# A graph layer on one core: the target list is loaded ahead of a row tile, its search is split in two sums, and the end of the last feature tile is dealt out anew

## The reference

```
h   = relu(layernorm(x))                      # x is (1250, 512)
xn  = batchnorm(h, g1, b1)
agg = segment_sum(xn[src], dst) / max(deg, 1)
conv = relu(agg @ W_conv + b_conv)
attn = (phi(q) @ (phi(k).T @ v)) / (phi(q) @ sum(phi(k))) @ Wo     # 8 heads, 256 features, the first 256 nodes
out = x + batchnorm(conv + attn + h, g2, b2)
```

## Time and the profile before

| | us |
|---|---|
| median of 3 runs | 176.44 (176.09 to 176.51) |
| the profiled execution | 176.07 |
| its span in the trace | 174.2 |
| TensorE busy | 165.6 (95%) |
| VectorE busy | 137.9 (79%) |
| ScalarE busy | 89.9 (52%) |

### The profile page before, as it was taken

The page is one execution under the profiler, slowest core; times in us unless marked ns, Lnnn a source line. Parts: engine busy times, 40 slices in busy tenths (PEclk is TensorE's granted clock), DMA queues, the critical chain, the costliest instruction groups (busy, mean ns, idle before and its releaser), DMA issues.

```text
span 174.2 us, 3024 instructions
## 1 busy us (share of the span) xinstructions
PE 165.6 (95%) x1131; PEld 108.9 (63%) x1132; DVE 137.9 (79%) x315; ACT 89.9 (52%) x163; POOL 7.6 (4%) x22
## 2 busy tenths in 40 slices
PE   7899999999999999999999999999999999999960
PEld 2388877545545546557777798684464574767940
DVE  2868889989947786999656785975999998597981
ACT  3426999839694779979416164217600505004050
POOL 5037000000000000000000000000000000000000
PEclk9999999999999999999999999999999999999998
DMA  5997970000610000000000000000294014050046
GB/s 186 362 328 185 346 261 0 0 4 0 218 43 0 4 0 0 0 4 2 0 4 0 0 4 0 0 4 4 70 336 186 0 28 119 6 147 0 4 124 172
DMA packets 11884, 13.71 MB, mean 79 GB/s; under 512 B 1458, under 2 KB 6748, under 8 KB 11868
## 3 DMA queue, kind: packets, MB, share of 16 engines
q1 hardware_dynamic: 10476, 12.13, 21.3%
q10 hardware_dynamic: 1072, 1.10, 1.8%
q0 software_dynamic: 320, 0.26, 0.7%
HBM read 10.92 MB, written 2.56 MB: 77 GB/s over the span
## 4 chain that ended last, share of the span: by engine, by line
PE 88%; DVE 3%; ACT 3%; DMA 2%; issue 1%; DVEq 0%; ACTq 0%
PE bank L978 24%; PE bank L708 20%; PE bank L638 8%; PE bank L659 4%; PE bank L732 4%; PE bank L722 4%; PE bank L751 4%; PE bank L685 4%; PE bank L650 3%; PE bank L630 3%; PE bank L1005 2%; PE bank L696 2%; DMA xs<-in_x 2%; DVE gl L1222 1%; DVE st L1054 1%
## 5 line engine op out<-in xcount | busy, mean ns | idle before, releaser
L978 PE MATMUL bank<-r,gh 128*128 128x512 f16 (+8 forms) x140 | 39.3, 314 | 0.0
L978 PE MATMUL bank<-r,gl 128*128 128x512 f16 (+8 forms) x140 | 39.3, 313 | 0.0
L708 PE MATMUL bank<-wc,xs 128*128 128x512 f32 (+1 forms) x80 | 38.5, 608 | 0.2 <-DVE gl L1222 0.2
L1085 DVE TENSOR_TENSOR ohb<-iota,bcol 128x1280 f16<-128x1280 f16 x25 | 20.5, 818 | 3.7 <-PE bank L650 3.7
L708 PEld LDWEIGHTS bank<-wc,xs 128*128 128x128 f32 (+1 forms) x80 | 13.6, 187 | 11.6 <-issue 11.6
L392 ACT ACTIVATE r<-bank 128x500 f16<-128x500 f32 x25 | 18.3, 764 | 3.4 <-PE bank L650 3.4
L978 PEld LDWEIGHTS bank<-r,gh 128*128 128x128 f16 (+1 forms) x140 | 13.5, 97 | 8.5 <-issue 0.3
L978 PEld LDWEIGHTS bank<-r,gl 128*128 128x128 f16 (+1 forms) x140 | 13.6, 97 | 8.2
L608 ACT ACTIVATE bw<-mv,epst 128x1 f32<-128x1 f32 x4 | 1.2, 295 | 31.0 <-DVE mv L1385 31.0
L638 PE MATMUL bank<-hT,r 128*128 128x256 f32 x64 | 14.5, 381 | 0.0
L650 PEld LDWEIGHTS bank<-ohv,ohb 128*128 128x128 f16 x250 | 9.7, 98 | 6.7 <-issue 5.3
(11 more groups left out here) (177 smaller groups left out, 267.1 us busy)
## 6 DMA issues: line engine op xcount, KB each, us to landing
xs<-in_x SPq DMA_DIRECT2D x15, 256.0 KB, 4.6
out<-xs SPq DMA_DIRECT2D x7, 256.0 KB
r<-in_L_gnn_Wq SPq DMA_DIRECT2D x1, 1024.0 KB, 7.5
r<-in_L_gnn_Wk SPq DMA_DIRECT2D x1, 1024.0 KB, 5.7
wc<-in_L_gnn_W_conv SPq DMA_DIRECT2D x1, 1024.0 KB, 9.1
wvo<-in_L_gnn_Wv SPq DMA_DIRECT2D x1, 1024.0 KB, 11.2
wvo<-in_L_gnn_Wo SPq DMA_DIRECT2D x1, 1024.0 KB, 5.3
xs<-in_x ACTq DMA_DIRECT2D x3, 256.0 KB, 4.2
```

The costliest lines, as they stand in the source:

```text
L708: last = nc.tensor.matmul(acc[0:n, :], xnT[:, f, i * P:i * P + n], wc[:, f, :], start=(f == 0), stop=(f == FT - 1))
L978: last = nc.tensor.matmul(acc[:, 0:cn], gg[0:n, s, f * P:(f + 1) * P], A16[0:n, s, c0:c0 + cn], start=(s == 0 and gg is gh), stop=(s == NT ...
L1085: last = V.tensor_tensor(oh[:, s0:s0 + n, :].rearrange("p s (m t) -> p s m t", t=2), iota16[:, 0:size].rearrange("p (m t) -> p m t", t=2). ...
```

## The change

Five edits at the start, and one at the end:

- ScalarE's queue issues the target list first and then tiles 3 and 5; SP issues tile 1 second, where the target list was. SP waits for tile 7, not 9, before `wk`.
- The thresholds are compared in three pieces: columns 0 to 3 ahead of `ln_stats(0)`, 3 to 5 between `ln_stats(0)` and `ln_scale(0)`, 5 to 10 after tile 1 is normalised. The wait for the target list thus stands ahead of the statistics of tiles 0 and 1.
- TensorE sums columns 0 to 5 between its first constant matmuls (now 15) and one more, and columns 5 to 10 after the turns of tiles 0 and 1; the three constant matmuls ahead of q are gone. VectorE adds the two sums (`first_rows` has three instructions instead of two).
- VectorE scales tile 1 (`normal_second`) without rectifying, and rectifies it as it copies the turned tile out of PSUM (`store_second`). ScalarE does neither for tile 1 any more.
- The last feature tile: VectorE scales columns 0 to 512, ScalarE 512 to 768, 768 to 1024 and 1024 to 1250; the parts of the third tile are turned in the order 2, 0, 1 instead of 1, 2, 0.

```diff
-ROUSE, ROUSE_MORE = 18, 3
+SEARCHED = 5
+ROUSE, ROUSE_LATE = 15, 1
...
-        order = [("hT", 0), ("hT", 1), ("first",), ("q", 0), ...
+        order = [("first",), ("hT", 0), ("hT", 1), ("q", 0), ...
...
-        order_end += [("agg", FT - 1, c) ...] + [("zT", FT - 2, j) for j in (1, 2, 0)]
+        order_end += [("agg", FT - 1, c) ...] + [("zT", FT - 2, j) for j in (2, 0, 1)]
...  SP
             load_x(0)
-            sp.dma_start(edst[:, :], dst...).then_inc(dst_in, 16)
+            load_x(1)
             sp.dma_start(wq, ...)
...
-            sp.wait_ge(x_in[NT - 1], 16)
+            sp.wait_ge(x_in[7], 16)
             sp.dma_start(wk, ...)
...  ScalarE
-            for i in (1, 3, 5):
+            act.dma_start(edst[:, :], dst...).then_inc(dst_in, 16)
+            for i in (3, 5):
                 act.dma_start(xs[:, i, :], x[i * P:(i + 1) * P, :]).then_inc(x_in[i], 16)
...
             ln_tile(0)
-            ln_tile(1)
             store_hT(0)
-            store_hT(1)
...
-                for a, b in (...) if f < FT - 1 else ((0, 256), (256, 512), (1024, N)):
+                for a, b in (...) if f < FT - 1 else ((512, 768), (768, 1024), (1024, N)):
...  TensorE
             rouse(ROUSE)
+            edge_search(0)
+            rouse(ROUSE_LATE)
             pe.wait_ge(id_set, 1)
             transpose_h(0)
             transpose_h(1)
-            edge_search()
-            rouse(ROUSE_MORE)
+            edge_search(1)
...
-            transpose_z(FT - 2, (1, 2))
+            transpose_z(FT - 2, (2,))
             turn_with_residual(FT - 2, 0)
+            transpose_z(FT - 2, (1,))
...  VectorE
+            def normal_second():
+                dve.wait_ge(ln_ready, 1)
+                V.tensor_scalar(xs[:, 1, :], xs[:, 1, :], lnw[:, 2, 1:2], lnw[:, 3, 1:2], ALU.mult, ALU.add).then_inc(n1_ready, 1)
+
+            def store_second():
+                acc = landed(dve, "hT", 1)
+                V.tensor_scalar(hT[:, :, P:2 * P], acc[:, :].rearrange("p (t n) -> p t n", t=FT), 0.0, None, ALU.max
+                                ).then_inc(read("hT", 1), 1)
...
+            dve.wait_ge(dst_in, 16)
+            link(V.tensor_copy(edst2[:, :, :], ...))
+            edge_thresholds(0, 3)
             ln_stats(0)
+            edge_thresholds(3, SEARCHED)
             ln_scale(0)
-            edge_thresholds()
+            normal_second()
+            edge_thresholds(SEARCHED, EJ // GR)
+            store_second()
             first_rows()
...
-                V.tensor_scalar(yT[:, f, 512:1024], yT[:, f, 512:1024], ...
+                V.tensor_scalar(yT[:, f, 0:512], yT[:, f, 0:512], ...
```

More of the change, by code:

```diff
@@ L118, in gnn_kernel @@
         edst2 = r2[0:EP, 1280:1280 + EJ // GR].bitcast(F16).rearrange("p (j t) -> p j t", t=2)
-        first = sb("first", [P, 2], F32)
+        first = sb("first", [P, 4], F32)
         rows = sb("rows", [P, 2], I32)
@@ L188, in gnn_kernel @@
         V_G1, V_B1, V_G2, V_B2, V_BC = range(5)
-        order = [("hT", 0), ("hT", 1), ("first",), ("q", 0), ("q", 1), ("hT", 2), ("hT", 3), ("hT", 4), ("hT", 5),
+        order = [("first",), ("hT", 0), ("hT", 1), ("q", 0), ("q", 1), ("hT", 2), ("hT", 3), ("hT", 4), ("hT", 5),
                  ("consts",), ("k", 0), ("hT", 6), ("hT", 7), ("hT", 8), ("hT", 9), ("dq",), ("k", 1), ("uk", 0), ("uk", 1),
@@ L201, in gnn_kernel @@
             order_end += [("agg", f, 0), ("agg", f, 1)] + [("zT", f - 1, j) for j in range(3)] + [("agg", f, 2)]
-        order_end += [("agg", FT - 1, c) for c in range(len(LAST_CHUNKS))] + [("zT", FT - 2, j) for j in (1, 2, 0)]
+        order_end += [("agg", FT - 1, c) for c in range(len(LAST_CHUNKS))] + [("zT", FT - 2, j) for j in (2, 0, 1)]
         order_end += [("zT", FT - 1, j) for j in range(3)]
@@ L261, in gnn_kernel @@
         h_ready = sem("h_ready")
+        n1_ready = sem("n1_ready")
         rows_ready = sem("rows_ready")
@@ L611, in _ @@
                 act.wait_ge(st2_ready, f + 1)
-                for a, b in ((0, 512), (512, 1024), (1024, N)) if f < FT - 1 else ((0, 256), (256, 512), (1024, N)):
+                for a, b in ((0, 512), (512, 1024), (1024, N)) if f < FT - 1 else ((512, 768), (768, 1024), (1024, N)):
                     act.activation(yT[:, f, a:b], yT[:, f, a:b], ACT.Identity,
@@ L626, in transpose_h @@
             def transpose_h(i):
-                pe.wait_ge(h_ready, i + 1)
+                if i == 1:
+                    pe.wait_ge(n1_ready, 1)
+                else:
+                    pe.wait_ge(h_ready, max(i, 1))
                 acc = pe_open(pe, "hT", i)
@@ L790, in rouse, with edge_search @@
                     nc.tensor.matmul(bank[0][:, :], cone[:, :], cone[:, 0:1].to_broadcast([P, 512]), start=True, stop=True)
-            def edge_search():
-                pe.wait_ge(nb_ready, 1)
-                acc = pe_open(pe, "first")
-                for hf in range(2):
[L796 to L799, removed]
+            def edge_search(half):
+                pe.wait_ge(nb_ready, half + 2)
+                if half == 0:
+                    pe_open(pe, "first")
+                acc = bank[uses[("first",)][0]]
+                a, b = ((0, SEARCHED), (SEARCHED, EJ // GR))[half]
+                for hf in range(2):
+                    for j in range(a, b):
+                        last = nc.tensor.matmul(acc[0:GROWS, 2 * half + hf:2 * half + hf + 1],
+                                                below[:, j, hf * GROWS:(hf + 1) * GROWS], cone[0:EP, 0:1],
+                                                start=(j == a), stop=(j == b - 1))
+                if half:
+                    last.then_inc(full("first"), 1)
             def project_consts():
@@ L1001, in transpose_z @@
                     for i in range(4 * j, min(4 * j + 4, NT)):
-                        if f == FT - 1 and i in (0, 2):
-                            pe.wait_ge(z_act, 3 * f + i // 2 + 1)
+                        if f == FT - 1 and i in (4, 6):
+                            pe.wait_ge(z_act, 3 * f + i // 2 - 1)
                         o = (i - 4 * j) * P
@@ L1088, in one_hots @@
                 last.then_inc(oh_ready, 1)
+            def normal_second():
[5 more added lines that the diff above has]
+                                ).then_inc(read("hT", 1), 1)
             def first_rows():
                 acc = landed(dve, "first")
-                V.tensor_scalar(first[0:GROWS, :], acc[0:GROWS, 0:2], -1.0, 0.0, ALU.add, ALU.max).then_inc(read("first"), 1)
+                V.tensor_copy(first[0:GROWS, :], acc[0:GROWS, 0:4]).then_inc(read("first"), 1)
                 stored(dve, "first")
-                V.tensor_scalar(rows[0:GROWS, :], first[0:GROWS, :], float(ROW_MAX), None, ALU.min).then_inc(rows_ready, 1)
+                link(V.scalar_tensor_tensor(out=first[0:GROWS, 0:2], in0=first[0:GROWS, 0:2], scalar=-1.0, in1=first[0:GROWS, 2:4],
+                                            op0=ALU.add, op1=ALU.add))
+                V.tensor_scalar(rows[0:GROWS, :], first[0:GROWS, 0:2], 0.0, float(ROW_MAX), ALU.max, ALU.min).then_inc(rows_ready, 1)
             def edge_values():
@@ L1242, in attn_norm, with edge_thresholds @@
                                 zr[:, i, :].unsqueeze(2).to_broadcast([P, 4, DH]), ALU.mult).then_inc(read("attn", i), 1)
[L1244 to L1249, removed]
+            def edge_thresholds(a, b):
+                shape = [EP, b - a, NW // 2, 2]
+                V.tensor_tensor(below[:, a:b, :].rearrange("p j (w t) -> p j w t", t=2),
+                                edst2[:, a:b, :].unsqueeze(2).to_broadcast(shape),
                                 thr16[0:EP, :].rearrange("p (w t) -> p w t", t=2).unsqueeze(1).to_broadcast(shape),
@@ L1256, in _ @@
             V.tensor_copy(win0[:, :], wbase_i[:, :])
+            dve.wait_ge(dst_in, 16)
+            link(V.tensor_copy(edst2[:, :, :], edst[:, ::GR].unsqueeze(2).to_broadcast([EP, EJ // GR, 2])))
+            edge_thresholds(0, 3)
             ln_stats(0)
+            edge_thresholds(3, SEARCHED)
             ln_scale(0)
-            edge_thresholds()
+            normal_second()
+            edge_thresholds(SEARCHED, EJ // GR)
+            store_second()
             first_rows()
```

6 lines of the change are left out of this document (3 added, 3 removed).

## The result

| | before | after |
|---|---|---|
| median | 176.16 (20 runs, 175.76 to 177.24) | 176.63 (20 runs, 176.11 to 179.27) |
| the profiled execution, span | 176.07, 174.2 | 178.52, 176.2 |
| mean granted clock of that execution | 0.996 | 0.987 |

A forecast was written before the change was run, and what follows sets the result against it. From the first matmul of q TensorE was taken as the bound, with VectorE's copy gating k. Start -0.88, list wait +1.23 and end -0.33 summed to +0.02, on a median of 176.44: 176.5, range 175.5 to 177.3.

The forecast's parts named there:

- The sum: Whole kernel: the three terms, -0.88 + 1.23 - 0.33, add up to +0.02 us, forecasting a median of 176.5.
- rule of t: Start: with the target list there at t, the first statistics and what follows shift by t - 3.37 us.
- Term 2: Start: waiting for the target list, there at t = 4.6, costs +1.23 us, from +0.1 to +2.1.
- rule of a tenth for a tenth: Start: every tenth of a microsecond by which the target list is late costs a tenth.
- case of the list crowded out: Start: tile 1 and `wq` pass beside the list, t 5.1 to 5.6, about 177.2; 0.30 with clock and lost gain.
- upper case of the prediction: Start: if DMA engines alternate between queues by single pieces, the list is there only at t = 5.5.
- Term 1: Start: were the list free, q could begin 1.19 us earlier and k, gated by VectorE, 0.88 earlier: -0.88.
- Term 3: End: the last residuals and the stores behind them come 0.33 us sooner: -0.33, between -0.1 and -0.45.
- rival of the clock: Start: TensorE's clock falls after some 2.5 us of pauses, lengthening q: +2, about 178.5; 5 in 100.
- `wk` at nothing: Start: `wk`, issued once tile 7 is there, lands sooner than before and stays hidden, costing nothing.

The follow-up runs named there:

- second execution: The changed kernel run once more, unchanged, on the chip of the next experiments: 176.30 (12 runs), ratio 1.0007 to the kernel before; this is its trace.
- filled kernel: Changed kernel with 20 instead of 15 constant matmuls at the start, 6 instead of 1 after the first half search, 1 more before q: 177.16, ratio 1.0064.
- copy moved alone: Kernel before with only VectorE's `query_copy(1)` moved ahead of the scale of tiles 6 to 9: 176.41 against 176.06, ratio 1.000.
- copy ahead with the old end: Changed kernel, old load order, list asked for later, `query_copy(1)` ahead of `ln_scale(2)`, without the edits of the end: 175.51, ratio 0.9949 to the kernel before.
- kernel with the copy ahead: Changed kernel with old load order, list waited for after tile 1's scaling, `query_copy(1)` ahead of `ln_scale(2)`: 175.24 against 176.16, ratio 0.9939.
- list later, new loads: Changed kernel with the list's wait behind `ln_scale(0)` and `normal_second`, both search halves behind the turns: 176.73, ratio 1.0037 to the kernel before.
- list second: Changed kernel with the old load order (list second on SP's queue), its wait still ahead of the first statistics: 179.39, ratio 1.0127 to the kernel before.
- list later, old loads: Changed kernel with the old load order, the list's wait after tile 1's scaling, both search halves behind the turns: 176.03, ratio 1.000 to the kernel before.

## Why the prediction was right, and which of its steps were off

The median of 176.63 stands beside a forecast of 176.5, but its composition is another. Executions whose clock held give 176.41 and 176.23, that is +0.25 and +0.07; the clock's fall adds 1.9 and 1.6 to about one execution in four, and 0.22 to the median of the first 20.

That the number came so near is in good part luck. The sum said +0.02, and +0.47 came. The 176.5 was counted from a median of three runs, 176.44, where 20 runs of the kernel before give 176.16: those 0.28 hide more than half of the miss. And the errors of the terms partly cancel: the start gave 0.21 less than forecast, the end 0.18 less, the falls cost 0.22 that stood at nothing, while the wait for the list was 0.27 shorter on the mean. That explains 0.34 of the 0.45 by which the sum was off; the rest stays open. What held is the mechanism of the first two terms: the wait for the list ahead of the first statistics moves everything behind it.

**The rule of t held.** The prediction's times shift with the first statistics. They came at 5.36, 1.29 later than 4.07, so the statistics of tiles 2 to 5 should start at 10.13 + 1.29 = 11.42 and q at 9.8 + 1.29 = 11.09. Measured were 11.39 and 11.11. In the second execution (t = 4.17, first statistics 4.87) 10.93 was due and 10.90 came. VectorE scaled tile 1 and copied its turned form as costed.

**Term 2, the wait.** t was forecast at 4.6; the traces with the list first show 4.66, 4.17, 4.51 and 3.97. The term of +1.23 is +1.29 in the profiled execution and about +0.96 at their mean of 4.33. The guess was sound for one execution, but t is no constant here, and its spread of 0.7 us is probably part of why the kernel after varies; how large a part was not measured. Nor does an early list pay in full. At t = 3.97 (four constant matmuls more) the statistics of tiles 2 to 5 were due at 10.13 + 0.60 = 10.73 and came at 10.87, because tile 2, whose load stands behind tile 1 and `wq` on SP's queue, was not there sooner:

```profile
2.14 8.71 DMA xs<-in_x
...
10.87 2.48 DVE st L1065 x4
```

The prediction's rule of a tenth for a tenth had no such end. The case of the list crowded out did not come: with single pieces by turns it would have been 5.5, and even as second on SP's queue it was 5.09. The Trainium skill, page "DMA: Bandwidth & Descriptors", section "Queues, rings and completion order", says that an engine takes the rows of queues by turns, a whole packet of several pieces at a time. The upper case of the prediction took single pieces, which the page does not state, and no trace bears it out.

**Term 1, the gain of the start, was 0.2 too large.** It was -0.88. The filled kernel shows it undisturbed by the clock: first statistics at 5.21, 1.14 late, so k was due at 19.15 + 1.14 = 20.29, and it began at 20.50. One tenth is the gap between the copy's end and k (0.15 measured, 0.05 assumed), the other the 0.1 that VectorE's list was later at tiles 2 to 5 (11.38 against 11.27) and still at the copy (ending 20.35 against 20.24). The term is -0.67. That VectorE and not TensorE's q decides k was right, and moving the copy ahead shows it from the other side: it gives back what the rest of that list costs.

**Term 3, the end, is right on the engines and mostly missing at the end of the span.** The last residual ends 0.33 sooner after the last aggregate, in the kernel after and in the end alone. But from aggregate to end of span the four traces with the old end (before, that without the third tile's stores, that with the copy moved alone, and the copy ahead with the old end) have 8.54 to 9.00, mean 8.76, and the ten with the new one 8.55 to 8.67, mean 8.61: 0.15, with a spread of 0.46 in the old ones. The prediction let the stream of stores move with the first of them. Which part does not move stays open: the third tile's stores were tried and are not it.

**The sum, corrected:** -0.67 + 0.96 - 0.15 = +0.14 where the clock holds, against +0.25 and +0.07 measured. For the kernel with the copy ahead the same account is 19.25 - 20.03 - 0.15 = -0.93, and 175.24 - 176.16 = -0.92 was measured. So close an agreement is luck: the traced spans differ by 0.7 only (173.5 against 174.2), because what lies between the start of k and the last aggregate, 145.34 us before, takes 145.34 to 145.86 in the 14 traces and took 145.55 in this one. The prediction had it run parallel.

**The rival of the clock failed in its premise and its chance, not in its price.** It named the three pauses of 2.5 us in all (1.1, 1.0 and 0.3 came, 2.4), and +2 us (q took 1.92 longer; k lost some 1.4 of it, since it would otherwise have waited for VectorE). But it gave 5 in 100, because "no pause of the start would be that long", by the end's 170.4 to 172.4 where the clock still showed 1.00. The fall came in 5 of 20 and 3 of 12 executions, and the two of them that were traced had no pause above 1.1 us. What was wrong was to ask for one long pause: short ones, with little work between, did it together. One pause alone was milder. By the one trace of each kernel, a single 1.3 us before the turns (copy ahead, old end) fell in none of 12, a single 1.5 (list later, new loads) in two of 11, and 1.7 and 1.0 (list second) in five of six. The kernel before is not wholly free of it either: of its 90 runs beside the experiments (without one of 961.73) two have fallen, with 178.21 at 0.985 and 177.59 at 0.988. Why one execution of the same kernel falls and the next does not stays open.

**`wk` at nothing** was true of the traced execution of before, where it came in time, and not of every one: 0.91 and 1.0 us were lost to it in two traces with the old order. The new order issued it at 13.34 and had it well before k. How often before pays for it is open, but the runs give a hint. Nine of its 90 have spans of 175.3 to 175.7 though their clock is 0.990 or more. Of the 78 runs whose clock held in the seven kernels with the new order of `wk` (the kernel after twice, four more constant matmuls, the list later with either loads, and the two with the copy ahead) none is longer than 174.9. So the one line that lets SP wait for tile 7 probably takes off this tail; no experiment changed it alone.

## What to carry to other kernels

Forecast a wait for a DMA as a spread and not as a moment, and keep it from standing ahead of work that does not need the data: here the same idea with the wait after the normalisation cost nothing, and became 0.6% faster once the copy that freed k's bank no longer stood behind a chain. When work is cut up so that the matrix engine waits several times in a row, add the pauses up and look at how little it does between them, since the clock's fall shows only in some executions; look at all runs and their clocks, not at the median alone. Gains ahead of a gate arrive only if the gate moves too, and the two edits must be tried together.

## What the runs showed of the hardware that was not expected

- The granted clock fell to 0.50 (1.2 GHz) at about the first matmuls of q, after waits of 1.1, 1.0 and 0.3 us with short matmuls between, and stayed there for some 3 us though TensorE was fully busy; with waits of 1.7 and 1.0 it was at 0.50 from 11 to 17 us. By their spans and clocks, about three executions of four of the same program did not fall.
- The PEclk column shows 1.00 from the start of the span, yet the constant matmuls of 512 columns start 0.43 us apart at first and 0.22 us apart later. The change came between 4.0 us (the kernel after once more) and 6.7 us (the list later, old loads), so the same 15 took 4.73 us in one execution and 5.75 in another, and this alone can open or close a pause behind them.
- The same 78 KB load, first on its queue, landed between 3.2 and 3.9 us after its issue in four executions, while tile 0 was on the other queue.
- From the last residual's end to the end of the span it takes 3.5 to 3.95 us, and finishing 0.33 sooner shortened the whole by 0.15 only, on the mean of the traces.
